# The last round of sums over h moved from GpSimd to VectorE, and the last tile's down projection reordered

## The reference

```python
W = weights[condition]                        # (32, 64, 64)
y = jnp.einsum('bct,bcd->bdt', x, W)          # x: (32, 64, 1024)

def oct_ternary_linear(xp, W):                # W: (8, out/8, in/8)
    Wq = ternary_dequant(W)
    M = jnp.einsum('jik,jod->koid', S_OCT, Wq)
    return jnp.einsum('...id,koid->...ko', xp, M)

h = silu(oct_ternary_linear(y, w_gate)) * oct_ternary_linear(y, w_up)   # 2732 hidden
out = x + oct_ternary_linear(h, w_down)
```

## Time and profile before

| | |
|---|---|
| median of 3 runs | 768.2 us (767.93 to 768.47) |
| the profiled execution | 768.18 us, its span 766.4 us |
| PE busy | 692.2 us (90%), 6934 matmuls |
| DVE busy | 519.6 us (68%) |
| POOL busy | 422.2 us (55%) |
| ACT busy | 336.3 us (44%) |

### The profile page before, as it was taken

How to read it: one execution, slowest core, us unless ns; L and a number is a source line. 1 busy time by engine, 2 the same in 40 slices (tenths; PEclk the granted TensorE clock), 3 DMA queues, 4 the chain that set the end, 5 groups by cost and what they waited for, 6 DMA issues and landing times.

```text
span 766.4 us, 16879 instructions
## 1 busy us (share of the span) xinstructions
PE 692.2 (90%) x6934; PEld 624.8 (82%) x6934; DVE 519.6 (68%) x830; ACT 336.3 (44%) x529; POOL 422.2 (55%) x448
## 2 busy tenths in 40 slices
PE   4259959899998999899998999899998999989994
PEld 3248948799897999789897999789897998988893
DVE  2859648566875678566875678566884668567846
ACT  4434746144452555245452554335451545334531
POOL 0200996664766356664766456764666347864560
PEclk9569989999999999999999999999999999999998
DMA  8200010031000210021000310021100300011001
GB/s 247 107 1 20 38 59 3 2 110 58 3 2 28 84 59 1 2 91 62 19 2 2 111 59 2 1 85 32 56 1 2 110 2 1 2 59 53 1 2 56
DMA packets 16703, 31.32 MB, mean 41 GB/s; under 512 B 3314, under 2 KB 10482, under 8 KB 16626
## 3 DMA queue, kind: packets, MB, share of 16 engines
q1 hardware_dynamic: 16626, 30.24, 11.9%
HBM read 21.84 MB, written 8.39 MB: 39 GB/s over the span
## 4 chain that ended last, share of the span: by engine, by line
PE 60%; POOL 19%; issue 9%; DVE 5%; ACT 5%; SPq 1%; DMA 0%; DVEq 0%; POOLq 0%
PE ps L918 49%; POOL z_f L505 8%; POOL h_pairs L505 8%; PE ps L995 7%; PE ps L905 3%; DVE z_op L780 2%; ACT z_op L606 2%; POOL down_u L505 2%; POOL z_op L505 1%; ACT h_op L591 1%; PE ps L912 1%; DVE o_sb L421 1%; POOL y_f L505 1%; ACT h_f L594 1%; DVE u_sb L785 1%
## 5 line engine op out<-in xcount | busy, mean ns | idle before, releaser
L918 PE MATMUL ps<-y_op,gate_table 128*128 128x256 f16 x2112 | 273.5, 275 | 13.7 <-DVE h_op L775 8.7
L918 PE MATMUL ps<-y_op,up_table 128*128 128x256 f16 x2112 | 271.9, 274 | 2.7 <-DVE up_table L718 2.7
L918 PEld LDWEIGHTS ps<-y_op,gate_table 128*128 128x128 f16 x2112 | 208.1, 99 | 39.8 <-DVE h_op L775 9.2
L918 PEld LDWEIGHTS ps<-y_op,up_table 128*128 128x128 f16 x2112 | 207.5, 98 | 28.1 <-DVE up_table L718 3.2
L505 POOL TENSOR_TENSOR h_pairs<-h_f 128x256 f32<-128x256 f32 x144 | 149.9, 1069 | 104.1 <-ACT h_f L594 100.3
L505 POOL TENSOR_TENSOR z_f<-h_pairs 128x512 f32<-128x512 f32 x96 | 129.7, 1372 | 99.2 <-DVE z_op L780 96.6
L618 ACT ACTIVATE ps<-ps,small 128x512 f32<-128x512 f32 x96 | 63.6, 662 | 164.3 <-DVE ps L785 122.8
L780 DVE TENSOR_TENSOR z_op<-z_f,z_op 128x1024 f16<-128x1024 f32 x48 | 61.8, 1288 | 86.9 <-ACT z_op L606 86.9
L995 PE MATMUL ps<-down_u,z_op 128*128 128x256 f16 x768 | 97.1, 285 | 19.6 <-DVE z_op L780 19.6
L421 POOL TENSOR_TENSOR o_sb<-o_sb,wd_sb 128x256 f32<-128x256 f32 (+1 forms) x140 | 81.6, 620 | 51.8 <-DVE wd_sb L830 50.7
L995 PEld LDWEIGHTS ps<-down_u,z_op 128*128 128x128 f16 x768 | 76.6, 102 | 31.9 <-DVE z_op L780 20.8
(11 more groups left out here) (72 smaller groups left out, 438.9 us busy)
## 6 DMA issues: line engine op xcount, KB each, us to landing
x_in<-in_x_dram SPq DMA_DIRECT2D x8, 1024.0 KB, 5.1
o_sb<-in_x_dram SPq DMA_DIRECT2D x16, 512.0 KB, 3.7
out_dram<-o_sb SPq DMA_DIRECT2D x16, 512.0 KB, 2.7
h_op<-in_L_ffn_w_gate_dram SPq DMA_DIRECT2D x3, 512.0 KB, 5.5
h_op<-in_L_ffn_w_up_dram SPq DMA_DIRECT2D x3, 512.0 KB, 5.5
z_op<-in_L_ffn_w_down_dram SPq DMA_DIRECT2D x1, 1364.0 KB, 9.2
cond_bd<-in_L_cond_weights_dram SPq DMA_DIRECT2D x32, 16.0 KB, 2.9
idx_sb<-in_itok_B_dram SPq DMA_DIRECT2D x1, 0.1 KB
```

The lines of the kernel that those rows point to most:

```text
L918: mm = pe.matmul(dst, table[m][:, slot, q, :], y_op[:, op, e, :], start=(i == 0 and e == 0), stop=(i == len(terms) - 1 and e == 1))
```

## The change

Three things change.

1. Round 5 of z leaves POOL. DVE does it (`last_round_of_z`) right after `h_lo` of chunk 11: 2 additions from `h_f` into a buffer that `p_sb` and `u_sb` now make up together, and 2 additions from there back into the v = 1 part of the last four chunks of `h_f`. Then DVE does `z_lo` of rounds 4 and 5, and only then `y_lo` of the next tile. Round 5 no longer waits for `z_f`.
2. In the last tile PE runs `last_down`: half 0 as before up to window 1, then u of windows 0 and 1 of half 1, c of window 2 of half 0, the wait for round 5, u of window 2 of both halves, and last all plain products of half 1, first those of bank c0 and then those of bank c1.
3. In the last tile POOL does `back` of half 0. DVE does `add_down` of half 0, `mix_down` of both, `back` of half 1 and then the two operations of `add_down` of half 1, one for each bank. SP stores half 0 whole, then half 1 in two pieces of 512 columns.

```diff
-        p_sb = sb("p_sb", [P, 2, TOK], F32)
-        u_sb = sb("u_sb", [P, 2, TOK], F32)
+        pu_sb = sb("pu_sb", [P, 2, 2, TOK], F32)
+        p_sb, u_sb = pu_sb[:, 0], pu_sb[:, 1]
...
+        z_dve = h_f[:, NC - 4:NC, 1, :]
+        def z_of(k):
+            return z_dve if k == NR - 1 else z_f[:]
...
+            store(NT - 1, 0)
+            for h in range(2):
+                cols = slice(h * D // 2, (h + 1) * D // 2)
+                sp.wait_ge(c_added, SUB * NT + h)
+                sp.dma_start(outr[rows(NT - 1, 1), cols], o_sb[:, 1, cols]).then_inc(out_stored[1], 16)
...
-                for k in range(2, NR):
+                for k in range(2, NR - 1):
                     round_of_z(T, k)
+            back(pool, NT - 1, 0)
...
+            def last_round_of_z(T):
+                dve.wait_ge(h_copied, NC * (T + 1))
+                dve.wait_ge(h_ready, NC * (T + 1))
+                pair_up(signed_add, NR - 1, pu_sb).then_inc(pairs_ready_dve, 1)
+                dve.wait_ge(pairs_ready_dve, T + 1)
+                signed_add(z_dve[:, 0:2], pu_sb[:, 0], pu_sb[:, 1], 1)
+                signed_add(z_dve[:, 2:4], pu_sb[:, 0], pu_sb[:, 1], -1).then_inc(z_ready_dve, 1)
...
                 h_lo(T, NC - 1)
+                last_round_of_z(T)
+                for k in range(len(Z_LO_AFTER), NR):
+                    z_lo(T, k)
                 if T + 1 < NT:
                     y_lo(T + 1)
-                for k in range(len(Z_LO_AFTER), NR):
-                    z_lo(T, k)
-                for s in range(SUB):
-                    add_down(T, s)
-                for s in range(SUB):
-                    mix_down(T, s)
-            for s in range(SUB):
-                back(dve, NT - 1, s)
+                if T + 1 < NT:
+                    for s in range(SUB):
+                        add_down(T, s)
+                    for s in range(SUB):
+                        mix_down(T, s)
+            T = NT - 1
+            add_down(T, 0)
+            mix_down(T, 0)
+            mix_down(T, 1)
...
+            back_to_outputs(dve, 1, 0).then_inc(o_mixed, 1)
+            dve.wait_ge(o_mixed, 1)
+            back_to_outputs(dve, 1, 1).then_inc(o_mixed, 1)
+            dve.wait_ge(o_mixed, 2)
+            for h in range(2):
+                add_down(T, 1, (h,))
...
+            def last_down(T):
+                n = NR * T
+                down_banks_free(T, 0)
+                pe.wait_ge(q_copied, NU * (T + 1))
+                for w in range(2):
+                    down_part(0, down_c_of(w), w == 0, False)
+                    pe.wait_ge(z_lo_ready, n + 2 * w + 2)
+                    down_part(0, down_u_of(w), w == 0, False)
+                down_banks_free(T, 1)
+                for w in range(2):
+                    down_part(1, down_u_of(w), w == 0, False, ("u0", "u1"))
+                down_part(0, down_c_of(2), False, True).then_inc(down_c_done, 1)
+                pe.wait_ge(z_lo_ready, n + NR)
+                down_part(0, down_u_of(2), False, True).then_inc(down_u_done, 1)
+                down_part(1, down_u_of(2), False, True).then_inc(down_u_done, 1)
+                for h in range(2):
+                    for w in range(NQ):
+                        mm = down_part(1, down_c_of(w, (h,)), w == 0, w == NQ - 1, (f"c{h}",))
+                    mm.then_inc(down_c_done, 1)
```

More of the change, by code:

```diff
@@ L376, in build @@
         z_ready = sem("z_ready")
+        pairs_ready_dve = sem("pairs_ready_dve")
+        z_ready_dve = sem("z_ready_dve")
         z_hi_ready = sem("z_hi_ready")
@@ L397, in pair_up @@
                     n = a.stop - a.start
-                    op = add(h_pairs[:, a, r0, :], h_f[:, c:c + 2 * n - 1:2, v, :],
+                    op = add(pairs[:, a, r0, :], h_f[:, c:c + 2 * n - 1:2, v, :],
                              h_f[:, c + 1:c + 2 * n:2, v, :], sign)
@@ L524, in round_of_z @@
                     pool.wait_ge(z_ready, n)
-                pair_up(signed_add, k).then_inc(pairs_ready, 1)
+                pair_up(signed_add, k, h_pairs).then_inc(pairs_ready, 1)
                 pool.wait_ge(pairs_ready, n + 1)
-                if n > 0:
-                    pool.wait_ge(z_lo_ready, n)
+                if k > 0:
+                    pool.wait_ge(z_lo_ready, NR * T + k)
+                elif T > 0:
+                    pool.wait_ge(z_lo_ready, NR * T)
                 signed_add(z_f[:, 0:2], h_pairs[:, 0], h_pairs[:, 1], 1)
@@ L592, in split_h @@
                 if T > 0 and c % 4 == 0:
-                    act.wait_ge(pairs_ready, NR * (T - 1) + 2 * (c // 4) + 2)
+                    act.wait_ge(pairs_ready, (NR - 1) * (T - 1) + min(2 * (c // 4) + 2, NR - 1))
+                    if c == NC - 4:
+                        act.wait_ge(z_lo_ready, NR * T)
                 act.activation(h_f[:, c], bank_r(s, 0), ACT.Copy).then_inc(h_copied, 1)
             def z_hi(T, k):
-                n = NR * T + k
-                act.wait_ge(z_ready, n + 1)
+                if k == NR - 1:
+                    act.wait_ge(z_ready_dve, T + 1)
+                else:
+                    act.wait_ge(z_ready, (NR - 1) * T + k + 1)
                 if T == 0 and k == 0:
@@ L605, in z_hi @@
                     act.wait_ge(down_c_ready, len(corr))
-                act.activation(z_op[:, k, 0], z_f[:], ACT.Copy).then_inc(z_hi_ready, 1)
+                act.activation(z_op[:, k, 0], z_of(k), ACT.Copy).then_inc(z_hi_ready, 1)
             def chunk(T, c):
@@ L795, in chunk @@
                     dve.wait_ge(u_ready, n)
-                signed_add(p_sb[:], bank_pr(s), q_sb[:], G2[K // 2] if K % 2 else 1).then_inc(p_ready, 1)
+                if T > 0 and c == 0:
+                    dve.wait_ge(z_ready_dve, T)
+                signed_add(p_sb, bank_pr(s), q_sb[:], G2[K // 2] if K % 2 else 1).then_inc(p_ready, 1)
                 if c > 0:
@@ L811, in chunk, with add_down @@
                                          op0=ALU.mult, op1=ALU.mult).then_inc(h_ready, 1)
-            def add_down(T, s):
+            def add_down(T, s, halves=(0, 1)):
                 n = SUB * T + s
                 dve.wait_ge(residual_loaded[s], 16 * (T + 1))
-                dve.wait_ge(down_c_done, n + 1)
+                dve.wait_ge(down_c_done, n + 1 + (halves[0] if T == NT - 1 else 0))
                 o = o_sb[:, s, :].rearrange("p (h k o) -> p h k o", h=2, k=4)
-                for h in range(2):
+                for h in halves:
                     last = dve.scalar_tensor_tensor(out=o[:, h], in0=down_banks(s)[f"c{h}"], scalar=down_scale(T),
@@ L861, in _ @@
                 h_lo(T, NC - 1)
+                last_round_of_z(T)
+                for k in range(len(Z_LO_AFTER), NR):
+                    z_lo(T, k)
                 if T + 1 < NT:
                     y_lo(T + 1)
-                for k in range(len(Z_LO_AFTER), NR):
-                    z_lo(T, k)
-                for s in range(SUB):
-                    add_down(T, s)
-                for s in range(SUB):
-                    mix_down(T, s)
-            for s in range(SUB):
-                back(dve, NT - 1, s)
+                if T + 1 < NT:
+                    for s in range(SUB):
+                        add_down(T, s)
+                    for s in range(SUB):
+                        mix_down(T, s)
[3 more added lines that the diff above has]
+            mix_down(T, 1)
+            dve.wait_ge(residual_loaded[1], 16 * NT)
+            dve.wait_ge(wd_ready, SUB * NT)
+            back_to_outputs(dve, 1, 0).then_inc(o_mixed, 1)
[4 more added lines that the diff above has]
+                add_down(T, 1, (h,))
         @block.tensor
@@ L987, in down_u_of, with down_part @@
                             yield f"u{r // 2}", r % 2, z_op[:, 2 * w + v, e, r], down_u[:, w, v, r]
-            def down_part(s, products, first, last):
+            def down_part(s, products, first, last, names=("c0", "c1", "u0", "u1")):
                 banks = down_banks(s)
                 products = list(products)
-                begun = set() if first else {"c0", "c1", "u0", "u1"}
+                begun = set() if first else set(names)
                 ends = {bank: i for i, (bank, *_) in enumerate(products)}
@@ L998, in down_part, with down_banks_free @@
                 return mm
+            def down_banks_free(T, s):
+                done = NC * (T + 1)
+                pe.wait_ge(h_lo_ready, done - 1 + s)
+                pe.wait_ge(h_copied, done - 1 + s)
+                pe.wait_ge(u_ready, done - 1 + s)
+                pe.wait_ge(p_ready, done - 1 + s)
+            def last_down(T):
[17 more added lines that the diff above has]
+                    mm.then_inc(down_c_done, 1)
             def down(T):
@@ L1007, in down @@
                 for s in range(SUB):
[L1008 to L1011, removed]
+                    down_banks_free(T, s)
                     if s == 0:
                         pe.wait_ge(q_copied, NU * (T + 1))
-                    elif T + 1 < NT:
+                    else:
```

(5 more changed lines are left out.)

14 lines of the change are left out of this document (7 added, 7 removed).

## The result

The changed kernel takes 737.6 us (median of 4 runs, 737.23 to 737.88) against 768.34 us (4 runs beside it): a ratio of 0.960, 95% interval 0.9583 to 0.9617. The forecast was 738.9 us, with 736.8 to 743.5 as its range. The profiled execution has a span of 736.1 us.

What follows compares the result with a forecast made beforehand. The prediction took PE as the bound, with a 2.8 us hole per tile. From 768.18 us it took 19.6 (holes), 6.6 (clock) and 3.1 (last tile), giving 738.9 us, range 736.8 to 743.5.

Steps and rivals of the forecast that it cites:

- The holes: Ends of tiles 0 to 6: PE's 2.8 us wait for `z_lo` before the down products closes, 19.6 us in all.
- The clock: Ends of tiles 0, 2, 4 and 5: without PE idling the clock no longer falls, 4 x 1.66 = 6.6 us.
- Rival B: Tile ends: the holes go but the half rate stays in four of them, 745.5 us; chance 0.05.
- The conflict on DVE and POOL: Tile ends: DVE's additions and POOL's round 4 block each other, yet the hole closes with 3.9 us to spare.
- The last tile: Last tile: a new 1.5 us hole in PE's down, but less work behind it, a gain of 3.1 us.
- Rival C: Last tile: new hole, clock and POOL beside DVE eat the tail's gain, 742 us; chance 0.12.
- Rivals A and D: Next tile's start: DVE frees the bank late; A a little, about 746 us, chance 0.08; D slower than before, chance 0.02.
- Rival D: Next tile's start: DVE frees the first bank so late that the kernel gets slower, about 774 us; chance 0.02.

Runs made afterwards that it cites:

- the runs with a hole put back: Changed kernel with idle DVE additions between `y_lo` and the last `z_lo` at the seven tile ends: 764.68 us with four additions, 744.66 us with one.
- the run with the order alone: Kernel before the change, with the two `z_lo` ahead of `y_lo` on DVE and nothing else: 751.75 us, ratio 0.9784.
- the run with the last tile alone: Changed kernel, but all six rounds stay on POOL and `y_lo` stays first: 770.41, 771.3 and 772.34 us, ratio 1.0041.
- the run with one addition: Changed kernel with one idle DVE addition between `y_lo` and the last `z_lo` at the seven tile ends: 744.66 us.
- the third version of tile 0: Changed kernel; in tile 0 rounds 0 and 1 taken up after chunks 8 and 9, POOL's sums over y of tile 1 after round 3: 731.37 us.
- the first two versions: Changed kernel; tile 0 takes up rounds 0 and 1 after chunks 8 and 9: 735.76 us; with rounds 2 and 3 both after 11: 733.97 us.

## Why the prediction was right

**The holes.** All seven closed, by the steps named. The size was short: the term of 19.6 us measured 20.9. From the first u products of the end of tile 0 (148.39 before, 145.44 after) to those of tile 6 (672.65 and 645.16) the difference grows from 2.95 to 27.49 us; less four slow spells of 1.66 that is 20.85 for seven holes, 2.98 each. The view of waits counts idle time from the modelled end of the last matmul. But the next one may start 0.17 us before that (641.59 + 3.74 is 645.33, and the next starts at 645.16), and the row of the weight loads in the kernel before had it right:

```profile
672.64 3.39 PEld L995 LDWEIGHTS ps<-down_u,z_op 128*128 128x128 f16 x32 [2.98 <-DVE z_op L780]
```

Seven times 0.17 is 1.2 us. The whole forecast was 1.3 us too high, and that the two agree is in part luck: the last tile gave 0.3 us less than forecast, and the median of the changed kernel lies 0.3 us below its profiled execution.

**The clock.** 6.6 us, as forecast; the runs with a hole put back bear out the cause. Rival B is out: at the changed kernel's tile ends the clock never falls. In both kernels it also falls in tile 0, behind PE's wait of 6.9 us (granted clock 0.50 from 105.5 to 108 us, 16 matmuls in 3.2 us where 1.9 is usual). The prediction looked only from 153.7 us on; as this one is the same before and after, the sum did not need it.

**The conflict on DVE and POOL.** POOL's round 4 was to take 7.1 us beside DVE's round and took 7.2; DVE's round was to take 5.0 and took 4.1, since it didn't have to wait for a POOL addition of 512. Everything behind it was within 0.2 us of the forecast: 3.8 us to spare for z (3.9), 1.8 us for the bank (1.6). The turns are seen in the last tile too (the single additions above; 5.78 us beside POOL, 3.04 alone). The Trainium skill, page "SBUF — State Buffer", section "Who interferes with whom", states this as a lock that the later instruction waits for when DVE has two SBUF inputs and GpSimd reads SBUF. The trace agrees, with the 0.29 us above.

**The last tile.** A gain of 2.8 us (3.1 forecast): a wait of 1.48 us (1.5), DVE's last addition 0.2 us later than forecast, and 2.6 us from there to the end (2.45). The 32 products that wait for round 5 have 96 plain products and 64 on z ahead of them, as the order of the changed kernel and the prediction's sum have it; the "128 + 64" of the text on the change is wrong. Rival C is out.

**Rivals A and D** named the right next limit, the bank that `add_down` frees; the run with the order alone has it at 1.5 us for each tile. In the changed kernel it has 1.8 us to spare. (Rival D's last figure, by its own terms, is 738.9 + 7 x 4.9 = 773 us and not 774.) What the prediction did not see is that two ways lead to the closed hole: DVE's round alone does all of it, and a new order of DVE's list nearly so.

## What to carry to other kernels

When an engine is named as late, look at who runs beside it: POOL's rounds were late by 3.4 us because DVE's `y_lo`, not yet needed, read two SBUF operands at the same time. Ask what each engine in an in-order list could do first, and which bank or buffer is freed last; reordering DVE's list cost no work and got 25.4 of 27.8 us. Measure a hole from start to start, against a place where the same matmuls run without one, and add what the clock loses behind it.

## What was unexpected of the hardware

Holes of one length do not all have the same effect on TensorE's clock. Of 21 idle spells of 2.73 to 2.81 us at tile ends (seven each in the kernel before, in the run with the last tile alone and in the run with the hole put back) thirteen were followed by a fall to 1.2 GHz, which cost 1.66 us in twelve of them and 1.33 in one, and eight by none; in the run with the hole put back they took turns from tile to tile. None followed a shorter spell: the seven of 1.42 to 1.46 us in the run with the order alone, the seven of under 0.9 us in the run with one addition, the 1.48 us in the last down of the changed kernel, or the 1.82 us of the third version of tile 0. A fall followed each longer one: the 6.9 us in tile 0 before and after, the 5.9 and 4.4 us there in the first two versions, and the 4.8 us in the last down of the run with the last tile alone. No spell lay between 1.82 and 2.73 us, and what decides it at 2.8 us was not settled.
